# A decoder layer in fp32: attention operands built on chip as FP32R row stacks, masked row maxima on DVE, an order per engine

## The reference

```
x = layernorm(x + self_attention(x))        # rope, causal, 16 heads of 8
x = layernorm(x + cross_attention(x, ctx))  # rope, 154 keys, no mask
x = layernorm(x + experts(x))               # 8 experts of 256, top 2, silu(x w1) * (x w3) @ w2

q = rope(x @ wq.T) @ wqi.T + bqi            # k and v alike; rope once before the inner projection
scores = q k^T / sqrt(8)                    # causal: -inf where key > query
o = softmax(scores) @ v;  return o @ out_w.T + out_b
```

## Time and profile before

| | us |
|---|---|
| median of 3 runs | 308.26 (307.1 to 312.71) |
| the profiled execution | 310.6 |
| its span, first to last instruction | 308.8 |
| PE busy | 273.9 (89%) |
| DVE busy | 184.1 (60%) |
| ACT busy | 131.0 (42%) |
| POOL busy | 107.8 (35%) |
| mean granted TensorE clock | 0.883 |
| DMA | 18.86 MB, 61 GB/s on average |

### The profile page before, as it was taken

The page is one execution under the profiler, slowest core; times in us unless marked ns, Lnnn a source line. Parts: engine busy times, 40 slices in busy tenths (PEclk is TensorE's granted clock), DMA queues, the critical chain, the costliest instruction groups (busy, mean ns, idle before and its releaser), DMA issues.

```text
span 308.8 us, 4423 instructions
## 1 busy us (share of the span) xinstructions
PE 273.9 (89%) x1488; PEld 140.5 (45%) x1488; DVE 184.1 (60%) x415; ACT 131.0 (42%) x239; POOL 107.8 (35%) x200
## 2 busy tenths in 40 slices
PE   7876789999999999697898968999999999999980
PEld 3333253454345544235442344534565655656650
DVE  1465667466797686326852287543387784676443
ACT  0400102587277675754437514467333334333220
POOL 9200011363135373544501013013255445564531
PEclk9996776599999999958577995599999999999997
DMA  7547606625105602262001500000000000001001
GB/s 238 106 133 180 162 11 160 181 72 140 38 13 116 208 4 70 66 174 71 4 2 55 153 2 3 5 2 0 2 0 0 0 2 0 0 2 36 0 0 34
DMA packets 10364, 18.86 MB, mean 61 GB/s; under 512 B 1413, under 2 KB 6853, under 8 KB 9845
## 3 DMA queue, kind: packets, MB, share of 16 engines
q1 hardware_dynamic: 9542, 17.04, 20.0%
q10 hardware_dynamic: 720, 1.28, 1.5%
q0 software_dynamic: 80, 0.26, 0.6%
HBM read 15.25 MB, written 3.13 MB: 60 GB/s over the span
## 4 chain that ended last, share of the span: by engine, by line
PE 69%; DVE 13%; ACT 5%; DMA 5%; issue 4%; POOL 1%; SPq 1%; POOLq 0%; ACTq 0%; DVEq 0%
PE psA L876 9%; PE psO L1034 8%; PE psO L938 6%; PE psB L904 6%; DVE negm L1303 5%; PE psO L944 3%; PE psB L782 3%; PE psB L910 3%; DMA bcol<-bcol_dram 2%; PE psJ L957 2%; PE psA L782 2%; PE psA L784 2%; PE psB L783 2%; PE psB L784 2%; PE psA L783 2%
## 5 line engine op out<-in xcount | busy, mean ns | idle before, releaser
L1303 DVE TENSOR_REDUCE negm<-psA 128x1 f32<-128x384 f32 (+5 forms) x136 | 78.9, 617 | 32.8 <-PE psA L876 16.1
L752 POOL TENSOR_TENSOR gated<-silu,wbc 128x512 f32<-128x512 f32 x32 | 41.0, 1284 | 50.9 <-DVE silu L1423 50.7
L1131 ACT ACTIVATE prob<-psB 128x512 f32<-128x512 f32 x80 | 45.2, 594 | 27.2 <-PE psB L904 13.9
L876 PE MATMUL psA<-kst,qst 72*128 72x128 bf16 (+3 forms) x128 | 34.4, 334 | 8.1 <-DVE negm L1303 4.1
L716 POOL CAST mpart<-negm 128x16 bf16<-128x16 f32 x16 | 3.5, 219 | 108.6 <-DVE negm L1303 85.0
L1191 ACT ACTIVATE silu<-psA 128x512 f32<-128x512 f32 x32 | 19.2, 599 | 44.7 <-PE psA L784 43.8
L904 PE MATMUL psB<-qst,kst 75*128 75x512 bf16 (+3 forms) x128 | 32.1, 340 | 1.4 <-ACT prob_more L1131 0.6
L1423 DVE SCALAR_TENSOR_TENSOR silu<-silu,psA 128x512 f32<-128x512 f32 x32 | 22.0, 686 | 16.9 <-ACT silu L1191 16.8
L1034 PE MATMUL psO<-hid,w 128*128 128x512 f32 x64 | 31.9, 603 | 0.1
L1434 DVE TENSOR_TENSOR hid<-psB,gated 128x512 f32<-128x512 f32 x32 | 22.0, 688 | 10.9 <-PE psB L784 10.0
L1131 ACT ACTIVATE prob_more<-psB 128x512 f32<-128x512 f32 x40 | 23.0, 594 | 8.4 <-PE psB L904 8.2
(11 more groups left out here) (154 smaller groups left out, 454.3 us busy)
## 6 DMA issues: line engine op xcount, KB each, us to landing
qst<-scr_q SPq DMA_DIRECT2D x8, 288.0 KB
stage<-w_dram SPq DMA_DIRECT2D x8, 256.0 KB, 3.3
kst<-scr_k SPq DMA_DIRECT2D x18, 96.0 KB
qst<-scr_q SPq DMA_DIRECT2D x2, 864.0 KB
scr_q<-part SPq DMA_DIRECT2D x12, 128.0 KB, 1.8
w<-w_dram SPq DMA_DIRECT2D x1, 1024.0 KB, 5.0
scr_k<-part SPq DMA_DIRECT2D x6, 128.0 KB
kstc<-scr_c SPq DMA_DIRECT2D x3, 240.0 KB
```

The lines of the kernel that those rows point to most:

```text
L752: nc.gpsimd.tensor_tensor(gated[:, n % 2, :], silu[:, n % 2, :], wbc[:, (E * b + f // 2) % 2, :], ALU.mult).then_inc(s_sg, 1)
L876: last = nc.tensor.matmul(ps[:, m * width:(m + 1) * width], qst[0:ROWS, b, h, 128 * i:128 * i + 128], keys, start=m == 0, stop=st == 1 and ...
L1131: nc.scalar.activation(dst, src, ACT.Exp, scale=SCALE).then_inc(b_done[n % 2], 1)
L1303: nc.vector.tensor_reduce(negm[:, u % 2, :, :].rearrange("p i j -> p (i j)")[:, c:c + nb], psA[n % 2][:, 0:nb * width].rearrange("p (m w) ...
```

## The change

Nearly the whole kernel body is touched. What it does:

- q and k are split into two FP32R parts (`high` from ACT, `low` from DVE) and stay in SBUF. **SQ, SK, SC** (new) are pairs of FP32R matmuls with 0/1 matrices `fr` that pick, for the 4 heads of a unit, rows in the order high, high, low (queries) and high, low, high (keys) into row groups of 32 partitions: 24 rows a head. ACT copies the result to `qa`, `kst`, `kc`; two further rows are set to one through the bias. Nothing of it goes through DRAM.
- **A** takes one head a fill: in a masked unit 12 fills (tiles 0 and 1 together, 2, 3, for 4 heads), 8 in a cross unit, matmuls of 24 rows in the head's row group, into one of **three** psA banks. The mask matmul is gone: DVE's `tensor_tensor_reduce` adds the mask table and takes the minimum of the negated sum, one instruction for each of the 16 tiles. Cross units keep TENSOR_REDUCE, 8 of 308 columns.
- **MP**: POOL writes the maxima as two parts (2 instructions instead of 4) into a padded tile. **MT** is an identity FP32R matmul of `qa` (512 columns) plus four of the padded maxima (128 columns) summed in one bank; ACT copies the whole 128x512 to `qb`. No DMA.
- **B** reads `qb` and `kst` or `kc`, 26 rows a head, 12 fills in a masked unit. The tail of the context keys is one 128-row matmul with a block layout (KT) in place of four.
- psO has **one** bank: each PV waits for the copy of the unit before, and both sequences' F2 use the same bank, the second after the copy of the first (YE).
- The order is made by `schedule`, separately for each engine, stage by stage of an item, with the longest remaining way as the tie break. The PROBE is gone. Loads are cut up and reordered: the pick matrices and the mask are new, the ones and the scratch tensors are gone.

```diff
-ROWS = PARTS * PARTS * HD
-KR = ROWS + PARTS
+ROWS = 3 * HD
+KR = ROWS + 2
...
+SIZE = {"A": 3, "B": 2, "O": 1, "J": 2}
+Y_AFTER = (NU - NG - 2 if SIZE["O"] == 2 else NU - 1, NU - 1)
...
+def a_fills(u):
+    if unit(u)[0] == 0:
+        kinds = (((0, 0), (1, 128)), ((2, 0),), ((3, 0),))
+    else:
+        kinds = (((0, 0), (1, SC)), ((2, 0), (3, SC)))
+    return [(j, tiles) for tiles in kinds for j in range(G)]
...
+def schedule(table):
...
+        score = (begin, -way[key])
...
+        orders.setdefault(engine[key], []).append(item)
...
-                        sp.dma_start(part_out(w, b, a), part[:, n % 2, a, :]).then_inc(s_sw[n], 16)
-                elif kind == "STACK" and args[0] == 0:
...
-                    q_rows(0, b, n)
...
-                    k_rows(b, n)
...
-                    sp.dma_start(qst[ROWS:ROWS + PARTS, b, G * g:G * g + G, :], mrow[:, u % 2, :]).then_inc(s_mr[u % 2], 16)
...
+                    link(nc.gpsimd.tensor_copy(rows[:, :, :, ROWS], negm[:, p, :, :]))
+                    nc.gpsimd.tensor_tensor(rows[:, :, :, ROWS + 1], negm[:, p, :, :], rows[:, :, :, ROWS].bitcast(FP32),
+                                            ALU.subtract).then_inc(s_mp, 1)
...
+            def select(ps, n, g, cols, pick_high, pick_low):
+                rows = slice(32 * g, 32 * g + 32)
+                nc.tensor.matmul(ps, fr[rows, pick_high, :], high[rows, n % 2, cols], start=True, stop=False)
+                return nc.tensor.matmul(ps, fr[rows, pick_low, :], low[rows, n % 2, cols], start=False, stop=True)
...
+                    j, tiles = a_fills(u)[k]
+                    rows = slice(32 * j, 32 * j + ROWS)
+                    for m, (i, c) in enumerate(tiles):
+                        width = 128 * (i + 1) if st == 0 else SC
+                        keys = kst[rows, b, g, 0:width] if st == 0 else kc[rows, g, b, :]
+                        last = nc.tensor.matmul(ps[:, c:c + width], qa[rows, b, g, 128 * i:128 * i + 128], keys,
+                                                start=m == 0, stop=m == len(tiles) - 1, skip_group_check=True)
...
-                        last = nc.tensor.matmul(diag, iden16, c16[:, H_MA:H_MA + 128].unsqueeze(1).to_broadcast([128, nb, 128]),
-                                                start=False, stop=True, skip_group_check=True)
...
+                    nc.tensor.matmul(ps[:, :], fr[:, FR_ID, :], qa[:, b, g, :], start=True, stop=False, skip_group_check=True)
+                    for i in range(QT):
+                        last = nc.tensor.matmul(ps[:, 128 * i:128 * i + 128], mpad[:, u % 2, i, :], fr[:, FR_ID, :], start=False,
+                                                stop=i == QT - 1, skip_group_check=True)
...
+                        nc.tensor.matmul(ps[:, :], kt_sb[:, b, g, :], qb[:, u % 2, :], start=True, stop=True)
...
+                            rows = slice(32 * j, 32 * j + KR)
+                            keys = kst[rows, b, g, 128 * kt:128 * kt + 128] if st == 0 else kc[rows, g, b, 0:128]
...
-                            pe.wait_ge(s_po, u - 1 if u < NU - NG else u)
+                        if u >= po_back(u):
+                            pe.wait_ge(s_po, u - po_back(u) + 1)
...
+                    if f == 0:
+                        pe.wait_ge(s_po, Y_AFTER[b] + 1)
+                        if b >= SIZE["O"]:
+                            pe.wait_ge(s_yT, b)
...
+                    free(JOB[item], nc.scalar.activation(qa[:, b, g, :], ps[:, :], ACT.Copy))
...
+                    free(JOB[item], nc.scalar.activation(qb[:, u % 2, :], ps[:, :], ACT.Copy))
...
+                    if st == 0:
+                        for i, c in tiles:
+                            width = 128 * (i + 1)
+                            last = nc.vector.tensor_tensor_reduce(
+                                out=junk[:, p, c:c + width], in0=psA[p][:, c:c + width], in1=c32[:, C_MASK + S - width:C_MASK + S], scale=-1.0,
+                                scalar=BIG, op0=ALU.add, op1=ALU.min, accum_out=negm[:, u % 2, i, j:j + 1])
```

More of the change, by code:

```diff
@@ new lines, in tasks @@
+        add("MP", (u,), [("POOL", 0.5)], [("A", (u, len(fills) - 1))] + ([(("MT", (u - 2,)), 0)] if u >= 2 else []))
+        add("MT", (u,), [("PE", 0.5), ("ACT", 0.5)], [("MP", (u,))],
+            [(1, (("B", (u - 2, len(b_fills(u - 2)) - 1)), 0))] if u >= 2 else [])
+        for k, blocks in enumerate(b_fills(u)):
+            cols = sum(S - 128 * kt for kt, _, _ in blocks) if st == 0 else S
+            deps = [("MT", (u,))] + ([("KT", ())] if st == 1 and k == NG else [])
+            late = [(1, ("PV", (u - 2, 2 if unit(u - 2)[0] == 0 else 1)))] if u >= 2 and k == 0 else []
+            add("B", (u, k), [("PE", 0.6 * cols / 2300.0 if k < 4 or st == 0 else 0.24), ("ACT", act(cols))], deps, late)
@@ new lines, in tasks @@
+        if st == 0:
+            for kt in (0, 1, 3, 2):
+                add("MK", (u, kt), [("POOL", 0.72)], [("B", (u, exps_of(u, kt)[-1]))])
+            pv = [(kt, us, [("MK", (u, kt)), ("VH", (b,))]) for kt, us in ((0, 0.86), (1, 0.65), (3, 0.22), (2, 0.43))]
+        else:
+            pv = [(kt, 0.86, [("B", (u, exps_of(u, kt)[-1])), ("CV", ())]) for kt in range(2)]
+        back = po_back(u)
+        for kt, us, deps in pv:
+            if u >= back:
+                deps.append(("POC", (u - back,)))
+            add("PV", (u, kt), [("PE", us)], deps)
@@ L722, in _ @@
+                pool.wait_ge(s_zero, 5 + j + 1)
+            for item in ORDER["POOL"]:
+                kind, args = item
+                if kind == "XB":
                     pool.wait_ge(s_xtok, 16)
@@ new lines, in _, with loaded @@
+            pe.wait_ge(s_warm, 1)
+            for _ in range(WARM):
+                nc.tensor.matmul(psO[-1][:, 0:320], warm[:, 384:512], warm[:, 0:320], start=True, stop=True)
+            waited = set()
+            def loaded(ready, count):
+                if ready.name not in waited:
+                    waited.add(ready.name)
+                    pe.wait_ge(ready, count)
+            for item in ORDER["PE"]:
+                kind, args = item
+                if kind == "U":
+                    b, w = args
+                    if b == 0:
+                        loaded(s_x0, 32)
+                    else:
+                        loaded(s_x1, 16)
```

1130 lines of the change are left out of this document (478 added, 652 removed).

## The result

The changed kernel takes 354.99 us (median of 4 runs, 349.28 to 359.95) against 308.34 us for the kernel before on the same chip (4 runs): ratio 1.137, 95% interval 1.1295 to 1.1445. I had forecast 275, with 252 to 306 as range. Executions of one kernel differ in the granted clock and by some per cent in time: a median here is that of all of them, a ratio compares those that were not slowed, where the record has one, and the profiled execution of the changed kernel is one of its slower ones (358.5 us, the fastest 349.28).

A forecast was written before the change was run, and what follows sets the result against it. TensorE was taken to bound the masked stage, with attention losing time to DRAM trips, ramp and lower clock. Setup 15.5, ramp 13, masked 90, cross 68, experts 88.6 sum to 275.1 of span, forecast 275 us, range 252 to 306.

The forecast's parts named there:

- masked stage's 90: Masked stage: 81.5 us before plus 14 of added TensorE work gives 95.5, less 5.5 of clock loss won back: 90 us.
- cross stage's 68: Cross stage: 53 us of full-clock work plus 18 for 8 units, overlap -5, idle +2: 68 us against 77.9.
- rival 4: Ramp and attention stages: the clock stays down behind 24-row matmuls in short fills; 50 us at 1.2 GHz gives 325; chance 0.12.
- a clock under 0.8 in the cross stage: Cross stage: a granted clock this low was named as a sign that would make the forecast wrong.
- Overlap, a quarter: Masked stage: matmuls in different row groups overlap, saving 1.3 us a unit, a quarter of the 2.6 for all overlapped.
- rival 1: Masked and cross stages: row groups overlap fully and per-engine orders close the gaps, 255 us; chance 0.12.
- Ramp, 13: First maxima to first product: DVE-paced maxima 7.8 us, split and sum 1.9, exponentials 2.4, mask 0.9; 33.6 falls to 13.
- Setup, 15.5: Start to first maxima: without the DRAM writes and stack reads 15.5 us, 10.3 less; bounds 14.5 and 19.
- rival 3: Maxima, scores and MT: narrow FP32R matmuls cost f32's price, 0.24 us for 128 columns, not 0.11; +33, 308 us; chance 0.12.
- Rival 2: Masked stage: DVE becomes the bound, as each masked maximum needs a second instruction of 0.18 us; 287 us; chance 0.14.
- One output bank at nothing: Masked stage: products wait for the previous unit's copy (0.6 + 0.4 us), but other work can fill it; worst 8 us.
- Experts and tail, 88.6: Expert stage and tail: 90.1 us before, less 1.5, with a little more of F1 running early: 88.6 us.

## Why the prediction was wrong

**The step that failed is the clock in the two attention terms of the sum.** The masked stage's 90 took 5.5 of its 6.5 us of clock loss back, and the cross stage's 68 is work at full clock with 2 us of idle time. Measured, the two stages ran at 0.55 and 0.63, which cost 95 us; 128 rows in A and B and nothing else brought 1.00 and 0.95. The reason that I gave for the high clock, rival 4's "against", fails with it. I had seen what matters (24 of 128 rows, 150 us of work, each us at the lower level costing one more) and dismissed it with nine slices of 9s, which were made by matmuls of 72 and 75 rows and so say nothing of 24. Rival 4 came true, also in the sign that I had named, a clock under 0.8 in the cross stage; I priced it at 50 us of work at 1.2 GHz and 325. (Rival 4 also spoke of short fills with waits between, and that part is not what the runs show: TensorE was busy for 97%.)

The span of 356.8 is 81.7 us over the 275.1 of the sum. Estimates from each stretch and its clock split this: the masked and cross stage lose 95 us to the clock and the ramp 6, and the work of the three comes to 73, 60 and 21 us where I had 90, 68 and 13. Setup is 1.8 over, experts and tail are 4.4 under.

Point by point:

- *Masked and cross stage, 90 and 68:* measured 132.6 and 95.8. With 128 rows at full clock they are 96.2 and 69.6. The difference of the two kernels, 36.4 + 26.2 = 62.6, less 2.2 in the ramp and 1.3 in setup, is all of the 59.1 us between the spans of 356.8 and 297.7.
- *Overlap, a quarter:* too little. 132.6 us at 0.55 is 73 us of work at full clock, an estimate, against 96 in full rows. On this estimate rival 1 was right on the sharing, and the clock hid it. The change does both at once: it lets heads share the array, and it takes the clock away.
- *Ramp, 13:* measured 26.9, the second wrong term. I moved 7.7 us of batch 1's projections into the masked stage; the order left them, and ten picks (4.6 us at 0.46 each), before the first product, and the clock of 0.77 cost 6 us. By TensorE's busy 28.7 of 29.1 us in the run with plain maxima, VectorE's pace, on which I had built the term, was not the limit.
- *Setup, 15.5:* measured 17.3, inside its bounds of 14.5 to 19.
- *FP32R of few columns at 0.11 us, rival 3:* the rate was right. In the timeline of the changed kernel, at a granted clock of 1.00, four of 128 columns take 0.56 us including the run-out of the last:

```profile
37.13 0.56 PE L778 MATMUL psJ<-fr,mpad 128*128 128x128 f32 x4
```

- *Rival 2:* refuted by 82 ns an accumulator read, and by 298.1 against 299.7 us without them.
- *One output bank at nothing, three banks for maxima at nothing:* together some 12 us in favour of the change at full clock, with the orders that go with them.
- *Experts and tail, 88.6:* measured 84.2.

In the run with 128 rows (a span of 297.7) my sum is still 23 us short: 16 of it the ramp (5 by its clock), 6 the masked stage, 3 setup, 2 cross, less 4 at the end, and this in full rows, which share nothing.

## What to carry to other kernels

Before a contraction is cut into row groups, count the rows that all matmuls of a stage use, and look in the trace for a stretch that used as few: a stretch of wide matmuls at full clock says nothing of narrow ones. Here sharing the array took the masked stage's work from 96 to 73 us at full clock, some 40 us at the clock that was granted (96 us at 0.55 are 175, measured 132.6), but only while every score matmul of the stage was narrow; mixing wide with narrow lost it, gave little of the clock back, and cost 0.29 us a change at 1.2 GHz. A term of the form "this work moves to another stage" must be checked against the order of the engine that does it.

## What was not expected of the hardware

- Rows in use decide the granted clock in this kernel, with TensorE busy for 97% or more of the masked stage: 0.55 at 24 and 26 rows, 0.74 at 64, 0.95 at 96 (in its fastest execution), 1.00 at 128. Rows whose keys are zero count (0.88 and 0.97 in that stage at 128 rows).
- 88 extra wide matmuls among narrow ones cost 98.9 us and left the clock at 0.51; a change between narrow and full rows took 0.29 us there.
- Zeros written by DMA in 1 KB pieces out of a broadcast tile (336 KB) landed 10.4 and 13.7 us after GpSimd issued them. The same issued by ScalarE held its queue for 5.44 and 4.13 us.
